# The spread of u in row tiles of 64 rows in place of 32

## The reference, cut to what matters

```python
xc = silu(conv4(x @ in_proj) + conv_b)            # 128 inner channels per chunk
dt = softplus(dt_proj(x_proj(xc)) + dt_b)         # and B, C: 16 values a position
for t in range(1024):                             # for 128 channels x 16 states
    h = exp(dt[t] * A) * h + (dt[t] * xc[t]) * B[t]
    y[t] = (h * C[t]).sum(over the 16 states)
out = out_proj((y + xc * D) * silu(z)) + skip * chunk
```

## Time and profile before

| | us |
|---|---|
| median of 3 runs (4798.27 to 4822.26) | 4801.27 |
| the profiled execution | 4817.56 |
| its span, from first to last instruction | 4815.6 |
| VectorE busy | 4248.1 |
| TensorE busy (matmuls) | 4166.2 |
| POOL busy | 3427.9 |
| ScalarE busy | 2566.8 |
| mean granted clock of TensorE | 0.836 |

### The profile page before, as it was taken

One profiled execution on the slowest core, in us unless ns is written; L12 is line 12 of the kernel. 1 busy time (PEld: TensorE's weight loads), 2 busy tenths in 40 slices (PEclk: granted clock), 3 DMA queues, 4 the chain that ended last, 5 costly groups with the idle time before them and its releaser, 6 DMA issues. The chain is left out here.

```text
span 4815.6 us, 51269 instructions
## 1 busy us (share of the span) xinstructions
PE 4166.2 (87%) x13584; PEld 1334.1 (28%) x13584; DVE 4248.1 (88%) x3519; ACT 2566.8 (53%) x3144; POOL 3427.9 (71%) x2085
## 2 busy tenths in 40 slices
PE   3788989988898888988989888898988889889887
PEld 2222323222232322323223232232323223232221
DVE  2699998999989898898988989898898998989997
ACT  2465554555556455564655555555555555546553
POOL 2577776777777776776767767776777767767775
PEclk8787987889788797887979889797887978879886
DMA  1566575675756666575665756647466565666664
GB/s 47 138 167 175 131 183 136 178 181 134 180 134 175 161 159 171 134 184 144 171 167 127 190 136 182 174 129 179 129 177 169 149 171 140 173 153 164 176 165 116
DMA packets 217783, 752.19 MB, mean 156 GB/s; under 512 B 27400, under 2 KB 28816, under 8 KB 213392
## 3 DMA queue, kind: packets, MB, share of 16 engines
q1 hardware_dynamic: 217488, 748.65, 60.4%
HBM read 639.49 MB, written 75.50 MB: 148 GB/s over the span
## 5 line engine op out<-in xcount | busy, mean ns | idle before, releaser
L590 POOL TENSOR_TENSOR state<-state,c_all 128x1024 f32<-128x1024 f32 x1024 | 2396.4, 2357 | 409.8 <-DVE state L960 388.8
L960 DVE TENSOR_TENSOR_SCAN state<-dtb,ub 128x1024 f32<-128x1024 f32 x1024 | 2340.1, 2285 | 51.7 <-ACT dtb L764 6.0
L1184 PE MATMUL ub<-u,spr 32*128 32x512 f32 x4096 | 1355.5, 752 | 380.6 <-DVE state L960 361.7
L951 DVE TENSOR_TENSOR ub<-ub,b_all 128x1024 f32<-128x1024 f32 x1024 | 1244.5, 1215 | 223.4 <-PE ub L1184 170.7
L764 ACT ACTIVATE dtb<-dtb,a_neg 128x1024 f32<-128x1024 f32 x1024 | 1150.8, 1140 | 503.2 <-DMA dtb<-dt_scratch 443.9
L1184 PEld LDWEIGHTS ub<-u,spr 32*128 32x128 f32 x4096 | 345.0, 208 | 1300.2 <-DVE state L960 786.5
L1200 PE MATMUL yp<-state,gat 128*32 128x512 f32 x4096 | 681.8, 744 | 3.2 <-POOL state L590 3.2
L1053 PE MATMUL mb<-xs,wtap 128*128 128x512 f32 x512 | 325.3, 793 | 15.7 <-DMA xs<-xn 10.6
L509 POOL TENSOR_SCALAR e_x<-e_x 128x1024 f32<-128x1024 f32 x64 | 66.6, 1040 | 311.0 <-ACT e_x L640 309.7
L665 ACT ACTIVATE dt<-mb 128x512 f32<-128x512 f32 x128 | 76.1, 595 | 347.5 <-PE mb L1084 347.5
L657 ACT ACTIVATE e_x<-mb,col 128x512 f32<-128x512 f32 x128 | 87.9, 687 | 275.5 <-PE mb L1067 275.5
(11 more groups left out here) (130 smaller groups left out, 4797.1 us busy)
## 6 DMA issues: line engine op xcount, KB each, us to landing
dtb<-dt_scratch SPq DMA_DIRECT2D x1024, 512.0 KB, 4.7
xs<-xn SPq DMA_DIRECT2D x128, 256.0 KB, 5.2
b_all<-bc_scratch SPq DMA_DIRECT2D x64, 512.0 KB, 6.2
c_all<-bc_scratch SPq DMA_DIRECT2D x64, 512.0 KB, 7.6
xt<-in_x SPq DMA_DIRECT2D x16, 1024.0 KB, 7.0
x_scratch<-xt SPq DMA_DIRECT2D x16, 1024.0 KB, 6.8
dt_scratch<-dt SPq DMA_DIRECT2D x64, 256.0 KB, 2.9
dt_scratch<-dt SPq DMA_DIRECT2D x128, 128.0 KB, 3.3
```

The source lines that it names most:

```text
L590: pool.tensor_tensor(v, v, c_all[:, c % 2, :], ALU.mult).then_inc(gated, 1)
L951: dve.tensor_tensor(v, v, b_all[:, c % 2, :], ALU.mult).then_inc(bx_done, 1)
L960: dve.tensor_tensor_scan(state[:, g % STATES, :], dtb[:, k, :], ub[:, g % 2, :], 0.0, ALU.mult, ALU.add).then_inc(scanned, 1)
L1184: last = pe.matmul(ub[:, g % 2, h * HALF:(h + 1) * HALF], spr[lo:lo + 32, GROUP[g] % 4, :], u[lo:lo + 32, c % 2, h * HALF:(h + 1) * HALF], ...
```

## The change

The spread takes tiles of 64 rows. Its calls read all rows 0 to 63 or 64 to 127 of u, and the weights pick eight of the 64 rows where they picked eight of 32; the other 56 rows meet weights of zero. The result is the same. The weight tile has eight versions instead of four, so it is twice as large. No instruction is added, taken away or moved on any engine.

```diff
@@ build, tiles
-        spr = sb("spr", [P, 4, P])
+        spr = sb("spr", [P, 8, P])
@@ spread_u
-                    lo = (32 * (GROUP[g] // 4) + h * TURN) % P
-                    last = pe.matmul(ub[:, g % 2, h * HALF:(h + 1) * HALF], spr[lo:lo + 32, GROUP[g] % 4, :],
-                                     u[lo:lo + 32, c % 2, h * HALF:(h + 1) * HALF], start=True, stop=True)
+                    lo = (TURN * (GROUP[g] // 8) + h * TURN) % P
+                    last = pe.matmul(ub[:, g % 2, h * HALF:(h + 1) * HALF], spr[lo:lo + TURN, GROUP[g] % 8, :],
+                                     u[lo:lo + TURN, c % 2, h * HALF:(h + 1) * HALF], start=True, stop=True)
@@ kernel, weights
-    spread = np.zeros((P, 4, P), np.float32)
+    spread = np.zeros((P, 8, P), np.float32)
@@
-        for v in range(4):
-            spread[p, v] = place + 8 * v == p % 32
+        for v in range(8):
+            spread[p, v] = place + 8 * v == p % TURN
```

## The result

The changed kernel takes 4578.1 us (median of 4 runs, 4566.96 to 4587.39) against 4801.24 us before: a ratio of 0.952, with a 95% interval of 0.9489 to 0.9552. It is faster by 4.8%. The prediction was 4580 us. The profiled execution took 4585.13 us, with a span of 4583.2 us.

What follows compares the result with a forecast made beforehand. VectorE was taken as the bound, waiting for TensorE. From the profiled 4817.6 us, 185 + 28 + 10 less and 0.7 more gave 4595 us, or 4580 us as a median; range 4515 to 4770 us.

Steps and rivals of the forecast that it cites:

- VectorE is the bound and waits for a slow TensorE: In the 14-batch loop VectorE works 3709.29 us, idles 390.2 us, and waits 242.1 us for TensorE.
- The stretch at full busy and half clock: At 1921.4 to 1931.6 us TensorE is busy 10.20 of 10.20 us at clock 0.50, suggesting array share counts.
- The calls cost the same: A spread's two calls at 64 rows take 1.13 us together, as at 32 rows: cost 0.
- Successive spreads share row tiles: 18 pairs of spreads that ran side by side now follow one another: 0 on the path, at most 18 us.
- The setup: The load of the spread's weights grows from 256 KB to 512 KB: 0.7 us more, all on the path.
- The clock: TensorE's mean clock in the loop rises from 0.84 to between 0.90 and 0.94.
- What the clock is worth: Time gained from the higher clock, priced by the same chunks at different clocks: 185 us plus 28 us over 14 batches.
- the best rows of each chunk: Each chunk runs as its fastest profiled instance: 279.6 us a batch for 292.8, or 185 us over 14 batches.
- The slope: Chunk 0 gains 79 us per unit of clock, 4 us more at 0.90; half taken, 28 us over 14 batches.
- Rows don't count: Rival: TensorE's clock follows busy time, columns or nonzero weights, so almost nothing moves: 4802 us, at most 4820; chance 0.16.
- The wrong places: Rival: the higher clock comes to stretches with slack, leaving 25 to 110 us of gain: 4690 to 4776 us; chance 0.14.
- The slower rival: A spread's two calls run one after the other, 2.0 us instead of 1.13: above 5050 us; chance 0.04.

Runs made afterwards that it cites:

- experiment 4: The changed kernel with all spread weights set to zero, every instruction the same: 4571.46 us, 0.9505 of the kernel before.
- experiment 1: The kernel before with only the larger weight tile loaded (eight versions, 512 KB), spreads still 32 rows: 4820.84 us, 1.0008 of before.
- experiment 6: Pixel norm's matmuls stream 64 equal columns instead of one: 4550.2 and 4552.42 us on the changed kernel, 4741.29 us on the kernel before.
- experiments 2: The kernel before with 64-row spreads in only part of the units: half gives 4637.72 us (0.9653 of before), a quarter 4714.81 us (0.9818).

## Why the prediction was right

*VectorE is the bound and waits for a slow TensorE.* Right. VectorE's work stayed, its waits for TensorE in the loop fell from 242.1 to 50.4 us; the prediction said some 50. The "issue" time that the change was not to touch fell too, from 40.9 to 30.3 us.

*The stretch at full busy and half clock shows that the share of the array counts.* Right as far as rows go. Busy time alone had spoken for no change, which is how I read the Trainium skill ("TensorE: Matmul & The Clock Gate", section "What's actually happening"). The runs disagree: a quarter, half and all of the units raise the clock step by step with the same instructions, while TensorE's busy time in the loop falls from 3622.29 to 3294.87 us. The spread's values don't matter (experiment 4), and neither does the tile's load (1). What is not shown is that it is the share of the array as such. I did not separate the number of rows from the number of 32-row tiles at work, nor from the size of the row tile. A spread in four tiles of 32 rows, two of them with zeros, would need two tiles to write one PSUM bank at once, and was not tried.

*The calls cost the same.* Right: 1.13 us for four records at full clock, as the own_z row had shown.

*Successive spreads share row tiles.* Right, and hidden. This is the place of the earlier trace rows in batch 6 of the kernel after, in the order of time:

```profile
...
1976.55 1.99 PE L1184 MATMUL ub<-u,spr 64*128 64x512 f32 x8
1978.47 1.98 PE L1194 MATMUL yp<-xc,dd 128*128 128x512 f32 x4
...
```

Two spreads take 1.99 us in place of 1.14. The scan's multiply (line 951) starts 2.63 us after the first of them in both kernels, so nothing of the 0.85 us reaches VectorE. The rule of the Trainium skill that speaks for four tiles of 32 rows ("TensorE: Matmul & The Clock Gate", section "Part 3: Packing small matmuls — row/col tiling") holds for this pair, but there is one a batch.

*The setup.* Estimated at 0.7 us. VectorE's wait for the last load, before and after:

```profile
...
DVE wtap L980 <- DMA iot<-in_iota: 11.3, 1, 11.3
...
```

```profile
...
DVE wtap L980 <- DMA iot<-in_iota: 12.2, 1, 12.2
...
```

It is 0.9 us. The first scan starts 3.9 us later than before (154.8 for 150.8 us), and 1.9 us later with the load alone (experiment 1), so more than the load is in it. VectorE's waits for the matmuls of line 1168 in the first 160 us are 3.3 us longer in the changed kernel (20.4 for 17.1 us). These matmuls are the same in both and stand ahead of any spread, but from 88 to 105 us they had a granted clock of 0.67 in place of 0.80; why there, no run shows. It is made up for soon after: from the start to the first scan of batch 1 the changed kernel takes 418.5 us for 427.7.

*The clock.* Forecast at 0.90 to 0.94 in the loop, measured 0.93.

*What the clock is worth.* The sum was right, and its parts only roughly, so that part of the hit is luck. Forecast were 13.2 us a batch by the best rows of each chunk, and 2 us more from chunk 0; measured are 15.4 us.

- Chunk 0 was to come to 78.14 - 2 = 76.1 us at a clock of 0.90. Its mean is 78.06 us at 0.87, so this term was too large by 1.9 us. The slope held only roughly: by it 0.87 would give 76.6 us. Where the clock does come to 0.90, with the norm widened as well (experiment 6), the mean is 76.2 us.
- Chunks 1 and 2 came out better than their rows, at 74.80 us for 76.24 and 62.56 for 62.78. These rows were not yet their floor.
- Chunk 3 has 61.93 us for 62.48, but the row of 62.48 was misread. It is the chunk of batch 14, the last of the loop, which is some 3 us shorter than the others in every kernel (58.75 us after, where the others take 61.4 to 63.2). It was not the same work at another clock: the best of the other thirteen before took 65.1 us. That chunk 3 fell to that number all the same is chance.
- The first and last batch were given 5 us each. Their stretches, setup included, are 9.2 and 6.7 us shorter.

So the sum came out as well as it did because one term was too large by what the others were too small.

*The rivals.* "Rows don't count" fell with experiments 2 and 4. "The wrong places" did not come: the waits for similarities and the keep map fell from 42.7 and 26.2 to 17.9 and 14.2 us. Experiment 6 shows that this rival had a core, since the similarities were a place where the low clock still cost something after the change. The slower rival did not come: a spread takes 1.13 us at full clock, not 2.0.

## What to carry to other kernels

When TensorE is busy and its granted clock is low, ask how much of the array each matmul puts to work. Where calls run side by side in row tiles, try the widest tile that still lets them do so: here it cost no time at full clock (1.13 us for either size), though the added rows only meet zeros. Price it by stretches of the same work at different clocks in the one trace, and only where the bounding engine waits for TensorE. Make sure that it is the same work: the last round of a loop may not be, as chunk 3 of batch 14 wasn't. Thin matmuls just ahead of dense ones can be worth widening too; here that gave 66 us on the kernel before and 18 us on the changed one.

## What the runs showed of the hardware

All-zero weights of the spread hold the clock as high as real ones (0.928 over the span, beside 0.921 for the changed kernel). Two 64x128 float32 calls in the two halves of the array take 1.13 us together at 2.4 GHz, and two 128x128 calls take 1.98 us. With 64 columns streamed by the norm in place of one, the similarities that follow run at a clock of 1.00 in place of 0.87. What I had not expected is how early the gain comes: one wide spread in four brings 1.8% of time of the 4.8% that all bring.
